# Layer 0 of a two-layer transformer block: probabilities turned by VectorE blocks and DMA instead of TensorE, and scaled by 1/sum before the value product

## The reference

```python
# attention 0: x (4, 256, 256); 16 query heads, 8 key/value heads of 128; window 128
q = rope(rms_norm(einsum('btd,ndh->btnh', x, q_kernel), q_norm_scale))
k = rope(rms_norm(k, k_norm_scale))          # k, v from kv_kernel
mask = (j <= i) & (i - j < 128)
probs = softmax(where(mask, (q * 0.08838) @ k.T, min))
enc = einsum('bkgts,bskh->btkgh', probs, v)
out = einsum('btnh,nhd->btd', enc, out_kernel)
```

## Time and profile before

| | us |
|---|---|
| median of three runs | 687.75 (686.14 to 690.43) |
| the profiled execution, its own time | 687.28 |
| its span, first to last instruction | 685.4 |
| layer 0's loop, slots 11 to 58 | 61.20 to 249.58 |
| granted TensorE clock | 1.000 |

### The profile page before, as it was taken

The page is one execution under the profiler, slowest core; times in us unless marked ns, Lnnn a source line. Parts: engine busy times, 40 slices in busy tenths (PEclk is TensorE's granted clock), DMA queues, the critical chain, the costliest instruction groups (busy, mean ns, idle before and its releaser), DMA issues.

```text
span 685.4 us, 16439 instructions
## 1 busy us (share of the span) xinstructions
PE 671.9 (98%) x4369; PEld 603.4 (88%) x4369; DVE 575.1 (84%) x1755; ACT 441.4 (64%) x1741; POOL 362.5 (53%) x555
## 2 busy tenths in 40 slices
PE   7999999999999998999999999999999999999998
PEld 3789999999999997888888899999999999978887
DVE  6979999899899999887875898989898988796333
ACT  4888888888798886431436666666666666764222
POOL 5998888898889873200138963415142324027000
PEclk9999999999999999999999999999999999999999
DMA  6010210101020001100024657465656555100000
GB/s 245 2 48 2 108 48 2 47 0 46 1 108 31 31 8 71 47 0 1 16 91 91 143 123 174 105 148 123 140 119 148 127 125 136 32 1 1 1 31 32
DMA packets 127117, 47.23 MB, mean 69 GB/s; under 512 B 93520, under 2 KB 122064, under 8 KB 126928
## 3 DMA queue, kind: packets, MB, share of 16 engines
q1 hardware_dynamic: 103824, 34.49, 20.8%
q10 hardware_dynamic: 23232, 12.06, 5.9%
HBM read 34.28 MB, written 12.26 MB: 68 GB/s over the span
## 4 chain that ended last, share of the span: by engine, by line
PE 85%; DVE 6%; issue 3%; ACT 3%; DMA 2%; SPq 0%; POOL 0%; ACTq 0%; DVEq 0%; POOLq 0%
PE bank L528 12%; PE bank L958 12%; PE bank L415 11%; PE bank L520 11%; PE bank L547 6%; PE bank L383 5%; PE bank L449 5%; PE bank L455 4%; PE bank L376 4%; PE bank L1032 3%; PE bank L431 3%; PE bank L470 3%; PE bank L1036 3%; DVE x L713 1%; PE bank L1052 1%
## 5 line engine op out<-in xcount | busy, mean ns | idle before, releaser
L713 DVE SCALAR_TENSOR_TENSOR x<-bank,rinv,x 128x256 f32<-128x256 f32 x256 | 121.0, 473 | 3.3 <-PE bank L415 1.0
L691 ACT ACTIVATE probs<-scores,negmax 128x128 f32<-128x128 f32 (+1 forms) x256 | 117.8, 475 | 6.7 <-DVE negmax L760 5.8
L600 ACT CAST enc_hi<-bank 128x256 fp32r<-128x256 f32 x128 | 47.8, 374 | 75.1 <-PE bank L455 68.8
L843 POOL TENSOR_TENSOR a_hi<-raw_a,zero 128x384 fp32r<-128x384 f32 (+1 forms) x60 | 44.2, 737 | 70.8 <-PE bank L547 70.8
L315 POOL TENSOR_TENSOR ln_r<-ln_ve,neg_half 128x1 f32<-128x1 f32 x26 | 17.1, 656 | 117.3 <-DVE ln_ve L289 117.3
L724 DVE TENSOR_TENSOR enc_lo<-bank,enc_hi 128x256 fp32r<-128x256 f32 x128 | 53.9, 421 | 24.7 <-PE bank L383 16.0
L415 PE MATMUL bank<-b_hi,enc_hi 128*128 128x256 f32 x256 | 73.4, 287 | 0.5 <-DVE x L713 0.5
L415 PE MATMUL bank<-b_hi,enc_lo 128*128 128x256 f32 x256 | 72.1, 282 | 0.0
L415 PE MATMUL bank<-b_lo,enc_hi 128*128 128x256 f32 x256 | 71.7, 280 | 0.0
L861 POOL TENSOR_TENSOR rot_a<-rot_a,rot_b 128x384 f32<-128x384 f32 x64 | 64.8, 1012 | 8.4 <-DVE rot_b L831 7.2
L859 POOL TENSOR_TENSOR rms_r<-meansq,neg_half 128x3 f32<-128x3 f32 x64 | 54.9, 857 | 7.4 <-DVE negmax L760 2.2
(11 more groups left out here) (185 smaller groups left out, 2368.0 us busy)
## 6 DMA issues: line engine op xcount, KB each, us to landing
shuffle<-blocks ACTq DMA_DIRECT2D x57, 192.0 KB, 2.5
arrived<-shuffle SPq DMA_DIRECT2D x228, 48.0 KB, 2.2
raw_a<-in_wa SPq DMA_DIRECT2D x40, 192.0 KB, 3.1
raw_a<-in_wa SPq DMA_DIRECT2D x9, 512.0 KB, 4.3
raw_b<-in_wb SPq DMA_DIRECT2D x16, 256.0 KB, 2.8
hid_last<-in_wax SPq DMA_DIRECT2D x2, 512.0 KB, 5.2
w_a<-in_w2t SPq DMA_DIRECT2D x1, 1024.0 KB, 4.9
raw_b<-in_wdown SPq DMA_DIRECT2D x2, 512.0 KB, 3.3
```

The source lines that it names most:

```text
L600: nc.scalar.copy(enc[0][:, hh, b * D:(b + 1) * D], bank[O_BANK][:, 0:D]).then_inc(s["ehi"], 1)
L691: nc.scalar.activation(probs[:, c % 4, c0:c1], scores[:, c % 2, c0:c1], ACT.Exp, bias=negmax[:, c % 2, r:r + 1], scale=-1.0, accum_out=row ...
L713: nc.vector.scalar_tensor_tensor(out=x[:, m % 8, :], in0=output_bank(m)[:, hh * D:(hh + 1) * D], scalar=rinv[:, u, r:r + 1], in1=x[:, m % ...
```

## The change

In layer 0, units 0 to 55 are treated like this (`moved`, `normalized`); units 56 to 63 stay as they were, with TensorE transposes, plain fp32 value products and 1/sum at the end.

- 1/sum is taken for each unit, as the last step of DVE's slot c (`dve_norm`). In slot c+1 ACT multiplies the probabilities by it, in place, in two instructions of 128 and 256 columns (`act_scale`), behind the high part of the encoded unit and ahead of the squares. Then DVE transposes the blocks (`dve_blocks`), behind the residual add and ahead of the wait for the scores and of the low part of the encoded unit.
- SP sends the blocks of unit c and then fetches unit c-1 (`sp_slot0`); the weights' loads are put into SP's list behind that, and SP's loop is written out. The 1 MB load of w2t and the loads for feed-forward 0 come behind the last fetch.
- The value product is plain fp32 for all units and reads `arrived`. The three transposes, ACT's two copies of the turned probabilities, DVE's low part of them, and both parts of v are gone.
- The output products of both heads add up in one half of a PSUM bank (still six passes), alternately in OP_BANK and PT_BANK up to unit 50 (`LAST_OUTPUT_PT`), and one plain add puts them on x.
- The hardware loop begins at slot 9, not 11, and ends at 56.

```diff
-FIRST_SLOT, LOOP_FROM, LOOP_STEP, LOOPS, LAST_SLOT = -5, (11, 9), 16, 3, 70
+FIRST_SLOT, LOOP_FROM, LOOP_STEP, LOOPS, LAST_SLOT = -5, (9, 9), 16, 3, 70
 FIRST_TAIL = UNITS - 8 + 7
 TAIL_SLOT = UNITS - 4
 SECOND_OUTPUT_FROM, SECOND_OUTPUT_TQ = UNITS - 10, UNITS - 6
-FIRST_SPLIT, SPLIT_VALUES = (8, 0), UNITS - 8
+LAST_OUTPUT_PT = UNITS - 14
+SPLIT_VALUES = UNITS - 8
 SPLIT_SCORES = 8
-MOVED = UNITS - 7
+MOVED = (UNITS - 8, UNITS - 7)
 ...
-    return L == 1 and (it is not None or m < MOVED)
+    return it is not None or m < MOVED[L]
+
+
+def normalized(L, it, m):
+
+    return L == 0 and moved(L, it, m)
 
 
 def in_parts(L, it, m):
 
-    return it is not None or FIRST_SPLIT[L] <= m < SPLIT_VALUES
+    return L == 1 and (it is not None or m < SPLIT_VALUES)
 ...
+                one = normalized(L, it, m)
                 for h in range(2):
                     for i, (l, r) in enumerate(PASSES):
-                        mm = pe.matmul(output_bank(m)[:, h * D:(h + 1) * D], enc[l][:, h, t * P:(t + 1) * P],
-                                       b_w[slot][r][:, h * D:(h + 1) * D], start=i == 0, stop=i == 2)
+                        cols = slice(0, D) if one else slice(h * D, (h + 1) * D)
+                        mm = pe.matmul(output_bank(L, m)[:, cols], enc[l][:, h, t * P:(t + 1) * P],
+                                       b_w[slot][r][:, h * D:(h + 1) * D], start=i == 0 and not (one and h),
+                                       stop=i == 2 and not (one and h == 0))
 ...
-                need(pe, s["ptev"], it, m + 1)
+                if normalized(L, it, m):
+                    need_turned(pe, L, it, m)
+                else:
+                    need(pe, s["ptev"], it, m + 1 - (MOVED[0] if L == 0 else 0))
                 need(pe, s["vev"], it, m - hh + 2)
                 need(pe, s["elo"], it, m)
+                there = arrived[:, m % 4, :] if moved(L, it, m) else probs_t[:, m % 2, :]
                 if in_parts(L, it, m):
-                    need(pe, s["ptlo"], it, m + 1 - FIRST_SPLIT[L])
-                    need_pairs(pe, s["vlo"], it, (m - hh + 2 - FIRST_SPLIT[L]) // 2, 4)
+                    need(pe, s["ptlo"], it, m + 1)
+                    need_pairs(pe, s["vlo"], it, (m - hh + 2) // 2, 4)
                     for i, (l, r) in enumerate(PASSES):
-                        pe.matmul(bank[O_BANK][:, 0:256], v_part(L, l, m // 8 % 2, b)[:, vc:vc + DH], turned[L][:, r, m % 2, :],
+                        pe.matmul(bank[O_BANK][:, 0:256], v_part(l, m // 8 % 2, b)[:, vc:vc + DH], turned[L][:, r, m % 2, :],
                                   start=i == 0, stop=False, skip_group_check=True)
                 else:
-                    pe.matmul(bank[O_BANK][:, 0:256], v_plain(L, m // 8 % 2, 2 * b)[:, vc:vc + DH], probs_t[:, m % 2, 0:256],
+                    if L == 1:
+                        there = probs_t[:, m % 2, :]
+                    pe.matmul(bank[O_BANK][:, 0:256], v_plain(L, m // 8 % 2, 2 * b)[:, vc:vc + DH], there[:, 0:256],
                               start=True, stop=False, skip_group_check=True)
-                last = arrived[:, m % 4, 256:384] if L == 1 and in_parts(L, it, m) else probs_t[:, m % 2, 256:384]
-                pe.matmul(bank[O_BANK][:, 128:256], v_plain(L, m // 8 % 2, 2 * b + 1)[:, vc:vc + DH], last,
+                pe.matmul(bank[O_BANK][:, 128:256], v_plain(L, m // 8 % 2, 2 * b + 1)[:, vc:vc + DH], there[:, 256:384],
                           start=False, stop=True, skip_group_check=True).then_inc(s["pv"], 1)
 ...
+        def send_blocks(eng, L, it, c):
+
+            if live(it, c) and moved(L, it, c):
+                need(eng, s_blocks[L], it, c + 1)
+                eng.dma_start(shuffle[c % 4].rearrange("k p i -> p k i"),
+                              blocks[:, c % 2, :].rearrange("p (k i) -> p k i", k=3)).then_inc(s_sent[L][c % 2], 16)
+
+        def act_scale(act, it, m):
+
+            if live(it, m) and moved(0, it, m):
+                need(act, s_norm, it, m + 1)
+                nc.scalar.mul(probs[:, m % 4, 0:128], probs[:, m % 4, 0:128], rinv[:, m % 16, 0:1])
+                nc.scalar.mul(probs[:, m % 4, 128:384], probs[:, m % 4, 128:384], rinv[:, m % 16, 1:2]).then_inc(s_scaled, 1)
 ...
             if c <= TAIL_SLOT or L == 1:
                 act_encoded(act, L, it, c - 4)
+            if L == 0:
+                act_scale(act, it, c - 1)
 ...
+                if normalized(L, it, m):
+                    if hh == 0:
+                        need(dve, s["op"], it, m + 1)
+                        nc.vector.tensor_tensor(x[:, m % 8, :], output_bank(L, m)[:, 0:D], x[:, m % 8, :],
+                                                ALU.add).then_inc(s["opadd"], 1)
+                    return
 ...
+        def dve_blocks(dve, L, it, c):
+
+            if live(it, c) and moved(L, it, c):
+                if L == 0:
+                    need(dve, s_scaled, it, c + 1)
+                else:
+                    need(dve, at[1]["exp"], it, 2 * c + 2, 2)
                 if it is not None or c >= 2:
-                    need_sent(dve, it, c - 2)
-                nc.vector.transpose(blocks[:, c % 2, :], probs[:, c % 4, :]).then_inc(s_blocks, 1)
+                    need_sent(dve, L, it, c - 2)
+                nc.vector.transpose(blocks[:, c % 2, :], probs[:, c % 4, :]).then_inc(s_blocks[L], 1)
+
+        def dve_norm(dve, it, c):
+
+            if live(it, c) and moved(0, it, c):
+                need(dve, at[0]["exp"], it, 2 * c + 2, 2)
+                nc.vector.reciprocal(rinv[:, c % 16, :], rowsum[:, c % 16, :]).then_inc(s_norm, 1)
 ...
                 dve_turned_lo(dve, L, it, c - 3)
+                if L == 0:
+                    dve_blocks(dve, 0, it, c - 1)
                 dve_scores_wait(dve, L, it, c)
                 dve_enc_lo(dve, L, it, c)
                 dve_maxima(dve, L, it, c)
 ...
+            if L == 0:
+                dve_norm(dve, it, c)
+            else:
+                dve_blocks(dve, 1, it, c)
 ...
+            def fetch_turned(L, c):
+
+                need_sent(sp, L, None, c)
 ...
+            def sp_slot0(c):
+
+                if c < MOVED[0]:
+                    send_blocks(sp, 0, None, c)
+                if c >= 1:
+                    fetch_turned(0, c - 1)
+                if c % 8 == 4 and c // 8 + 3 < PAIRS + 2:
+                    load_a(0, None, c // 8 + 3, 0)
+                if c % 8 == 7 and c // 8 + 2 < PAIRS:
+                    load_b(0, None, c // 8 + 2)
+
+            load_a(0, None, 1, 0)
+            load_b(0, None, 1)
+            load_a(0, None, 2, 0)
+            for c in range(MOVED[0] + 1):
+                sp_slot0(c)
+                if c == 20:
+                    load_late(0)
+            sp.dma_start(w2_a[:, :, :].rearrange("p a d -> p (a d)"), w2t).then_inc(s_w2, 16)
+            for h in range(2):
+                sp.wait_ge(at[0]["b"], 28 + 4 * h)
+                sp.dma_start(raw_b[:, h, :], wdown0[h]).then_inc(raw_bs[0][h], 16)
```

More of the change, by code:

```diff
@@ L217, in build, with v_part @@
         turned = [turned0, sb("turned1", [P, 2, 2, 256], F32R)]
-        def v_part(L, part, slot, e):
-            if L == 0:
-                return b_w[slot][part][:, WB + e * DH:WB + (e + 1) * DH]
+        def v_part(part, slot, e):
             if e < 2:
@@ L246, in build @@
         s_out = sem("stored")
-        s_blocks = sem("L1_blocks")
-        s_sent = [sem(f"L1_blocks_sent{i}") for i in range(2)]
-        s_arrived = [sem(f"L1_turned_arrived{i}") for i in range(2)]
+        s_norm, s_scaled = sem("L0_norms"), sem("L0_probs_scaled")
+        s_blocks = [sem(f"L{L}_blocks") for L in range(2)]
+        s_sent = [[sem(f"L{L}_blocks_sent{i}") for i in range(2)] for L in range(2)]
+        s_arrived = [[sem(f"L{L}_turned_arrived{i}") for i in range(2)] for L in range(2)]
         def ffn_pieces(f):
@@ L347, in v_bank, with output_bank @@
             return bank[(TQ_BANK, PT_BANK)[m % 2]]
-        def output_bank(m):
+        def output_bank(L, m):
+            if L == 0 and m <= LAST_OUTPUT_PT and m % 2 == 0:
+                return bank[PT_BANK]
             if m < SECOND_OUTPUT_FROM or m % 2:
@@ L697, in dve_rinv @@
             s, m = at[L], c - 2
-            if live(it, m) and m % 2 == 0:
+            if live(it, m) and m % 2 == 0 and not normalized(L, it, m):
                 need(dve, s["exp"], it, 2 * m + 4, 2)
@@ L731, in dve_turned_lo @@
                 need(dve, s["ptev"], it, m + 1)
-                src = arrived[:, m % 4, 0:256] if L == 1 else bank[PT_BANK][:, 0:256]
-                nc.vector.tensor_tensor(turned[L][:, 1, m % 2, :], src, turned[L][:, 0, m % 2, :].bitcast(F32),
+                nc.vector.tensor_tensor(turned[L][:, 1, m % 2, :], arrived[:, m % 4, 0:256], turned[L][:, 0, m % 2, :].bitcast(F32),
                                         ALU.subtract).then_inc(s["ptlo"], 1)
-        def dve_blocks(dve, it, c):
-            if live(it, c) and moved(1, it, c):
```

(35 more changed lines are left out.)

74 lines of the change are left out of this document (27 added, 47 removed).

## The result

| | before | after |
|---|---|---|
| median of 20 runs each | 687.21 (686.01 to 690.43) | 690.51 (686.91 to 696.03) |
| profiled execution, its own time | 687.28 | 689.38 |
| its span | 685.4 | 687.6 |
| granted TensorE clock | 1.000 | 0.995 |

The ratio is 1.0046 (95% interval 1.0032 to 1.0061): 0.5% slower, inside the 1% that was called no change, and 1.5 over the forecast of 689.0. That two numbers lie near each other says little about the steps; the trace has to be read for them.

What follows compares the result with a forecast made beforehand. It took TensorE to bound the kernel before, a VectorE-ScalarE ring after. Loop -1.7, turns +2.2, DRAM and loads +0.5, start +0.5 make +1.5 on 687.28: 688.8, predicted as 689 us, range 680.5 to 696.

Steps and rivals of the forecast that it cites:

- TensorE's part: TensorE's loop slot: without transposes and with a plain product it loses 0.24 us and could run at 3.67.
- The ring: VectorE-ScalarE chain of 1/sum, scales, transpose, maxima, rotation: least slot 3.87 us instead of 3.906, loop gains 1.7.
- the bounds of the scales: Two prices for ScalarE's two scales, which no row showed: 0.56 us as copies, 0.82 as exp.
- exp's price: ScalarE's two scales priced as exp, 0.30 and 0.52 us, 0.82 together; taken for the forecast.
- the copies': ScalarE's two scales priced as copies, 0.15 and 0.405 us, 0.56 together; the lower bound.
- Where the loop turns: ScalarE's stop at each of two turns costs about 1.5 us instead of 0.35: +2.2 (0 to +3.4).
- The way through DRAM: Sends and fetches stay hidden behind the slots; late fetches and large loads sharing the queue cost +0.5 us (0 to +3).
- either case: Transfer through DRAM: hidden but for slow fetches and shared loads, +0.5 us, or longer than the ring, 4.0 a slot.
- Rival 2: TensorE's value product waits for turned units landing late: slot 4.0 us, total 695; chance 0.20.
- 1.3 us to spare: Margin hiding the path from value product through DRAM to the value product two units on: 6.4 us over two slots.
- The start: First unit's value product has no slots behind it to hide its fetch: +0.5 us (0 to +1.5).
- Rival 1: Scales as cheap as copies, so GpSimd's 3.735 us bounds the loop's slot: total 680.5; chance 0.20.

Runs made afterwards that it cites:

- e2: Changed kernel with the two late feed-forward loads issued at slots 18 and 26 instead of both at 20; 685.81 us.
- e6: e2 with the loop begun one slot earlier, at slot 8 instead of 9; 690.61 us.
- e3: Changed kernel with VectorE's block transpose moved behind both maxima and the two late loads apart at slots 18 and 26; 693.59 us.
- e7: e3 with ScalarE instead of SyncE issuing the send of unit c-1, behind its second exp; 686.82 us.
- e10: e7 with ScalarE's loop written out, the other engines keeping theirs; 678.65 us.
- e11: e7 with all engines' loop begun one slot earlier, at slot 8 instead of 9; 684.20 us.
- e5: Kernel before the change with layer 0's value product plain fp32 for all units, transposes and 1/sum at the end kept; 690.86 us.
- e8: e7 with the add of epsilon to the means of squares moved from GpSimd to VectorE; 690.14 us.
- e9: e2 with ScalarE instead of SyncE issuing the sends, the block transpose staying ahead of the scores; 694.54 us.
- e1: Changed kernel with VectorE's block transpose moved behind both maxima; 698.59 us.
- e4: e3 with the add of epsilon to the means of squares moved from GpSimd to VectorE; 693.61 us.
- e12: Kernel before the change with ScalarE's loop written out; 686.52 us.

## Why the prediction came true, step by step

- **TensorE's part: right.** There are no transposes in the loop, and the plain product takes 0.43 to the small one (151.48 to 151.91 in the trace), where 0.44 was forecast. TensorE alone could run at 3.66, and every second slot does.
- **The ring: right, in place and in size.** Forecast 3.87, measured 3.845; forecast -1.7, measured -2.2 (48 slots of 3.845 would give -2.9; slots 13 and 17 took some of it). The choice between the bounds of the scales decided it: 0.31 to the second scale and 0.49 for it, 0.80, by exp's price 0.82, by the copies' 0.56. What was a little off evened out: 0.13 from the end of the scale to the transpose where 0.04 stood, and 0.97 for 1.01. The Trainium skill ("ScalarE: Activation LUTs", What ACT_TABLE_LOAD costs) had given an estimated 0.29 + 0.49 = 0.78; the trace agrees with it, and with exp's row as closely.
- **Where the loop turns: wrong in the changed kernel.** Forecast +2.2 (its own terms, 2 x (1.5 - 0.35), give 2.3), measured -0.9, since the stops weren't there at all. The step that failed is that a stop seen in one program was carried over to another. e2 has none at either turn; e6, with the loop one slot earlier, has them, and a turn costs 2.7 and 2.4 there (10.38 and 10.11 less 7.69) where 1.5 was forecast, with a stop of VectorE beside ScalarE's.
- **The way through DRAM: wrong in size, and for another reason than either case named.** Forecast +0.5, with 0 to 3 as bounds; measured +4.8, nearly all of it one event: three loads in a row ahead of a fetch. The loads were counted, and that three of them would stand together wasn't priced. Rival 2's mechanism is the same wait, but it came in slots 13, 17 and 23 alone, not in most.
- **"1.3 us to spare": too much, and wrong as a sum.** In the changed kernel it held for most slots, but in slots 13 and 17 the value product waited without a load right ahead of its fetch. The sum left out VectorE's ordered queue and TensorE's scores: with the transpose behind them (e3) the path that closes through SyncE's list takes 8.6 over two slots.
- **The start: +0.5 forecast, +1.5 measured.** Slot 3 (4.32 for 3.35) and slot 9 (4.87 for 3.98) lose 1.9, others win 0.4 back; a fetch that lands late was forecast for the first unit alone. **Behind slot 58:** nothing forecast, -1.0 measured; no run tells why.
- **Rival 1** names the floor that e7, e10 and e11 reach, 3.74 to 3.75, and not the way there: cheap scales weren't needed, an open ring was.

So the total was right by luck in part. Against their forecasts the turns are -3.1, the loads +4.3, the start +1.0, the ordinary slots -0.5 and what is behind them -1.0, which nearly cancel: +0.7 (+2.2 for +1.5). TensorE's part and the ring were right by themselves.

## What to carry to other kernels

When work is taken off the bounding engine, follow each new handoff round until it comes back to the same engine one slot on, and add up the steps. Do it again for the queue that only issues DMAs: a fetch that stands behind the next unit's send is tied to everything that this send waits for (e3, e7). Spread loads that have no haste over slots, and ask what stands in the queue right behind them (e2). A stop where a loop turns belongs to one program: before a change of 1% is judged, see in both traces whether the stops are there.

## What the runs showed of the hardware

- At the long slot the clock that TensorE was granted fell to the lower of its two levels (1.2 and 2.4 GHz), after the engine had stood for 3.41. The windows of the changed kernel (stretch, length, busy of PE, PEld, DVE, ACT, POOL; clock, DMA share, GB/s):

```profile
106.00:113.00 7.00, 6.21 (x40) 5.43 (x39) 5.81 (x23) 6.53 (x31) 6.29 (x13) 1.00 0.90 271
113.00:118.00 5.00, 2.38 (x10) 2.20 (x10) 1.22 (x4) 0.71 (x4) 3.03 (x5) 0.77 0.66 125
118.00:122.00 4.00, 4.00 (x24) 3.67 (x24) 3.31 (x11) 2.79 (x15) 1.74 (x3) 0.86 0.38 82
```

The value product's two matmuls took 1.21 there in place of 0.60. Cut finer, the clock is 1.00 in 112.50:115.60, where TensorE does nothing, 0.53 in 115.60:117.00, 0.50 in 117.00:118.00 and in 118.00:119.00, where it is full, and 0.96 in 119.00:120.00. The engine was at work until 112.2, with the clock at 1.00.
- The first of these rows is the bunch of loads: the DMA engines 0.90 busy at 271 GB/s, where the loop's usual stretch has 0.59 and 132. The fetch behind the bunch took 2.87 to issue and the next send 1.55, where some 2.0 and 0.38 are usual.
- Engines stop 2.0 to 2.8 where their loop turns, or hardly or not at all, by where the loop lies: ScalarE in the kernel before, e5 to e8 and e9's second turn (it stands 3.79 at e9's first, which the profile puts down to TensorE); VectorE in e6 and e11 alone; neither in the changed kernel and e1 to e4. With ScalarE's loop written out (e10, e12) it has no such stop.
